# An expert layer on one NeuronCore: each group turned ahead of the output in front of it, and the last four results of a call copied by VectorE

## The chip, the cores and the metric

The kernel runs on one core of a Trainium2 chip. The metric is the device time of one execution in microseconds (us). Before the change it was 627.59 us, the median of three runs (627.01 to 629.43).

## What is computed

A block of six residual steps on x of shape (2, 1024, 128): a gated feed-forward, a softmax attention with eight heads, the feed-forward again, an expert layer, a linear attention (a delta scan with decay), and the expert layer again. The change touches the expert layer, which runs twice:

```python
logits = (x_flat @ Wr + br) / max(ROUTER_TEMP, 1e-06)
probs = jax.nn.softmax(logits, axis=-1)
topk_w, topk_idx = jax.lax.top_k(probs, TOP_K)
topk_w = topk_w / jnp.clip(jnp.sum(topk_w, axis=-1, keepdims=True), 1e-09)
h = jnp.einsum('nc,ech->neh', x_flat, W1) + b1
h = _layernorm(h, g1, be1)
h = jax.nn.gelu(h, approximate=False)
expert_out = jnp.einsum('neh,eho->neo', h, W2) + b2
sel = jnp.take_along_axis(expert_out, topk_idx[:, :, None], axis=1)
y_flat = jnp.sum(sel * topk_w[:, :, None], axis=1)
```

There are 16 experts, each token goes to 2 of them, and every width is 128.

## The kernel before

The two expert layers are called m3 (before the linear attention) and m5 (behind it, the last thing in the kernel). Each works on two halves of the tokens, m3[0] and m3[1], m5[0] and m5[1]. A half goes through these steps.

GpSimd scatters the half's rows by expert into a buffer in HBM, rows_in (16 indirect DMAs, `moe_pool_send`). SyncE loads the sorted rows in 8 groups (`moe_sync_load`). A group is 4 tiles of 128 rows, the eighth of a half has 3. The 16 groups of a call (both halves) are numbered u = 0 to 15 here. When all 8 groups of a half are stored to rows_out in HBM, GpSimd gathers the results with 16 indirect DMAs (`moe_pool_fetch`, line L1130), and VectorE adds them to x (`moe_vector_add`, L1369 and L1374), in four quarters that each wait for their 4 gathers.

For one group the engines do this, and each step waits for the one above it:

- PE `turn_in(u)` (L1174): 4 transposes of the loaded rows. ACT `rows(u)` (L1263) copies them out of PSUM.
- PE `hidden(u)` (L1191, L1193): a bias matmul and the first expert matrix. ACT `squares(u)` (L1270).
- DVE `summed`, `rstds`, `scaled` (L1327, L1338 with a chain of small operations, L1346): two groups share one chain of small operations: 0, then 1 and 2, ..., 13 and 14, then 15 alone.
- PE `turn(u)` (L1201): 4 transposes of the normalised group. ACT `gelu(u)` (L1280): 4 activations.
- PE `out(u)` (L1214, L1216): a bias matmul and the second expert matrix. ACT `out_in(u)` (L1289) copies the result out of PSUM, and ACT `store(u)` (L1154) issues its DMA to rows_out.

The order on each engine is written out by hand. PE does, for u = 0 to 12, `turn(u)`, `turn_in(u+4)`, `hidden(u+3)`, `out(u)`, and at the end 

```python
            turn(last - 3)
            turn(last - 2)
            out(last - 3)
            turn(last - 1)
            out(last - 2)
            out(last - 1)
```

ACT does `gelu(u)`, `store(u-1)`, `rows(u+4)`, `squares(u+3)`, `out_in(u)`. PSUM has 8 banks: 2 for turned-in rows, 4 for hidden groups, 1 for turned groups (TURN_BANK), 1 for outputs (OUT_BANK). Behind the groups of m3, VectorE runs `behind_m3`: the adds of m3[0] and the statistics for the linear attention. The first step of the linear attention on PE is L1484 (transposes of x; the second four wait for all four quarters of the adds of m3[0]), then L1491 and L1499. Behind the groups of m5, VectorE adds m5[0] and then m5[1], and SyncE stores x.

Of the kernel before, what the change touches and what calls it, by code (L numbers as in the profile page):

```python
# [20 lines left out]
P = 128  # L21
# [36 lines left out]
def build(nc, A):  # L58
    with ExitStack() as ctx:
# [3 lines left out]
        def sem(name):  # L63
            return ctx.enter_context(nc.semaphore(name))
# [842 lines left out]
        LEAD = 3  # L907
# [60 lines left out]
        class t:  # L968
# [1 line left out]
            xt, xtc = sem("t_rows_turned"), sem("t_rows_in")  # L970
            h, sq, sqr = sem("t_hidden"), sem("t_squared"), sem("t_squares_summed")
            z, zt, ac = sem("t_normed"), sem("t_normed_turned"), sem("t_gelu")
            y, yc = sem("t_out"), sem("t_out_copied")
            ys = [sem(f"t_out_stored{k}") for k in range(4)]
            yg = [sem(f"t_out_gathered{k}") for k in range(4)]

        def tiles_in(g):
            return min(4, NTL - 4 * (g % NGR))
# [170 lines left out]

        def moe_scalar_store(act, m, g):  # L1150
            b, u = m.b, NGR * m.i + g
            act.wait_ge(t.yc, u + 1)
# [10 lines left out]
        def moe_tensor(pe, pair, between):  # L1163
# [33 lines left out]
            def turn(u):  # L1197
                g = (u - u0) % NGR
                pe.wait_ge(t.z, u + 1)
                for j in range(tiles_in(g)):  # L1200
                    ins = pe.transpose(ps[:, turn_bank(last - u), j * P:(j + 1) * P], t_z[:, u % 4, j, :], cc("ident"))  # L1201
                ins.then_inc(t.zt, 1)

            def out(u):
                m, g = pair[(u - u0) // NGR], (u - u0) % NGR
                k = tiles_in(g)
                pe.wait_ge(t.ac, u + 1)
                bank = out_bank(last - u)
                if u == last - 1:
                    pe.wait_ge(t.yc, u - 1)  # L1210
                elif u >= u0 + 1 and u != last - 2:
                    pe.wait_ge(t.yc, u)
# [18 lines left out]
                hidden(u)  # L1231
                between(u - u0)
            routed(pair[1])
            for u in range(u0, last - LEAD):
                turn(u)
                if u + LEAD + 1 < last:
                    turn_in(u + LEAD + 1)
                hidden(u + LEAD)
                out(u)
            turn(last - 3)  # L1240
            turn(last - 2)
            out(last - 3)
            turn(last - 1)
            out(last - 2)
            out(last - 1)

        def turn_bank(left):

            return TURN_IN_BANKS[0] if left == 2 else TURN_BANK

        def out_bank(left):
            return TURN_IN_BANKS[1] if left == 2 else OUT_BANK

        def moe_scalar(act, pair, between):
            u0 = NGR * pair[0].i
# [28 lines left out]
            def out_in(u):  # L1284
                k = tiles_in(u)
                act.wait_ge(t.y, u + 1)
                if u >= 4:
                    act.wait_ge(t.ys[u % 4], 16 * (u // 4))
                nc.scalar.activation(t_y[:, u % 4, 0:k, :], ps[:, out_bank(last - u), 0:P * k].rearrange("p (j f) -> p j f", f=P), ACT.Copy)\  # L1289
                    .then_inc(t.yc, 1)  # L1290

            for u in range(u0, u0 + LEAD + 1):
                rows(u)
# [15 lines left out]
            gelu(last - 3)  # L1309
            store(last - 4)  # L1310
            gelu(last - 2)
            out_in(last - 3)
            gelu(last - 1)
            store(last - 3)
            out_in(last - 2)
            store(last - 2)
            out_in(last - 1)
            store(last - 1)

        def moe_vector_tiles(dve, vs, pair, behind):  # L1320
            u0 = NGR * pair[0].i

            def summed(u):
                k = tiles_in(u)
                dve.wait_ge(t.sq, u + 1)
                at, pos = place(u)
                nc.vector.tensor_reduce(t_ss[:, at, pos:pos + k], t_sq[:, u % 2, 0:k, :], AX.X, ALU.add).then_inc(t.sqr, 1)  # L1327

            def place(u):

# [20 lines left out]
            for u in range(u0 - 1, last + 1, 2):  # L1351
# [893 lines left out]
        def _(pe):  # L2245
# [48 lines left out]
            pe.wait_ge(t.yc, 2 * NGR)  # L2294

            def turned_before(g):
                pe.wait_ge(l.y, 2)
# [93 lines left out]
```

## Time and profile before

| | |
|---|---|
| median of 3 runs | 627.59 us (627.01 to 629.43) |
| the profiled execution: its own time, its span | 628.28 us, 626.1 us |
| PE busy | 512.6 us (82%) |
| VectorE busy | 484.3 us (77%) |
| ScalarE busy | 327.0 us (52%) |
| GpSimd busy | 142.0 us (23%) |
| groups of m3, from the first `turn` to the end of the last `out` | 350.1 to 407.1 us of the span |
| groups of m5, likewise | 537.9 to 595.5 us of the span |

The profiled execution's time is 2.18 us more than its span, and 0.69 us above the median. In the rows below "ACTq" and "SPq" are DMA issues on ScalarE's and SyncE's sequencers, "PEclk" is the granted clock of TensorE as a share of 2.4 GHz, and the square bracket at the end of a row is the idle time of the engine in front of it and what ended that.

### The profile page before, as it was taken

What the parts mean: (1) busy time and instruction counts of PE and PEld (TensorE: products, weight loads), DVE (VectorE), ACT (ScalarE), POOL (GpSimd) and SP (SyncE); (2) the same over time, 40 slices, a digit from 0 to 9 for tenths busy, and PEclk for the clock granted to TensorE, in tenths of its full rate; (3) what the DMA queues carried; (4) which work ended last, traced back from release to release, by engine and by line L of the source; (5) the groups of instructions that cost most, each with busy time, mean ns of one, the idle gap of its engine ahead of it and who ended that gap; (6) DMA issues with size and microseconds to landing.
All of it is one profiled execution on the core that took longest, in us unless ns stands there. A gap on an engine that the chain in (4) does not pass through costs nothing.

```text
span 626.1 us, 9476 instructions
## 1 busy us (share of the span) xinstructions
PE 512.6 (82%) x3033; PEld 270.7 (43%) x3033; DVE 484.3 (77%) x1373; ACT 327.0 (52%) x645; POOL 142.0 (23%) x188
## 2 busy tenths in 40 slices
PE   7687979989999999899585899877797786899800
PEld 3452322322223222244252777665555454777600
DVE  6997989898888998686987666897888758666722
ACT  2345546866676676798132688744242102678700
POOL 3000020000000000000075703654000072713645
PEclk9776969999999999999786899998797878899955
DMA  5006400028815000000225295421000015273432
GB/s 202 1 1 157 91 1 1 18 67 152 248 65 136 3 1 2 1 3 2 76 106 157 87 276 154 122 64 34 2 2 1 0 58 152 70 215 85 132 95 67
DMA packets 55981, 48.62 MB, mean 78 GB/s; under 512 B 5758, under 2 KB 48190, under 8 KB 55678
## 3 DMA queue, kind: packets, MB, share of 16 engines
q1 hardware_dynamic: 35326, 31.31, 18.4%
q0 software_dynamic: 4224, 8.59, 4.8%
q10 hardware_dynamic: 16384, 8.13, 4.5%
q8 instruction: 25, 0.41, 0.3%
q14 instruction: 22, 0.18, 0.1%
HBM read 24.94 MB, written 20.60 MB: 73 GB/s over the span
## 4 chain that ended last, share of the span: by engine, by line
PE 49%; DVE 25%; issue 9%; POOL 7%; ACT 4%; DMA 4%; SPq 1%; POOLq 0%; ACTq 0%; DVEq 0%
PE ps L747 7%; PE ps L716 7%; PE ps L737 7%; POOL rows_in L1105 5%; DVE arena L803 4%; PE ps L1193 4%; PE ps L1216 4%; POOL arena L1130 2%; PE ps L1555 2%; PE ps L1174 2%; PE ps L1201 2%; DVE stat L249 1%; ACT arena L1687 1%; PE ps L1499 1%; PE ps L545 1%
## 5 line engine op out<-in xcount | busy, mean ns | idle before, releaser
L803 DVE TENSOR_REDUCE arena<-ps 128x1 f32<-128x512 f32 x256 | 162.2, 682 | 25.4 <-PE ps L716 25.0
L869 ACT ACTIVATE arena<-ps 128x512 f32<-128x512 f32 x256 | 138.3, 603 | 58.5 <-PE ps L737 57.1
L716 PE MATMUL ps<-arena 96*128 96x512 bf16 x256 | 98.4, 397 | 7.9 <-DVE arena L803 6.8
L737 PE MATMUL ps<-arena 99*128 99x512 bf16 x256 | 96.4, 388 | 3.3 <-DMA arena<-arena 2.7
L1105 POOL DMA_INDIRECT rows_in<-xl,route x64 | 62.6, 978 | 149.9 <-DVE route L1061 131.6
L1130 POOL DMA_INDIRECT arena<-rows_out,route x64 | 61.3, 957 | 78.9 <-DMA rows_out<-arena 52.2
L747 PE MATMUL ps<-arena 128*32 128x512 f32 x512 | 68.2, 605 | 0.6 <-ACT arena L869 0.4
L737 PEld LDWEIGHTS ps<-arena 99*128 99x128 bf16 x256 | 24.9, 99 | 73.9 <-ACT arena L869 48.9
L716 PEld LDWEIGHTS ps<-arena 96*128 96x128 bf16 x256 | 25.1, 99 | 51.7 <-DVE arena L803 34.5
L1280 ACT ACTIVATE arena<-ps,route 128x128 f32<-128x128 f32 x124 | 46.4, 460 | 1.3 <-PE ps L1201 1.2
L1327 DVE TENSOR_REDUCE arena<-arena 128x4 f32<-128x512 f32 (+1 forms) x32 | 21.2, 663 | 30.4 <-ACT arena L1270 30.3
L884 POOL CAST arena<-arena 128x16 bf16<-128x16 f32 x7 | 1.4, 196 | 171.5 <-issue 148.4
L1193 PE MATMUL ps<-w,arena 128*128 x248 | 39.1, 303 | 0.0
L1216 PE MATMUL ps<-w,arena 128*128 x248 | 37.8, 297 | 0.0
L1193 PEld LDWEIGHTS ps<-w,arena 128*128 128x128 f32 x248 | 32.5, 204 | 7.9 <-issue 7.9
L1216 PEld LDWEIGHTS ps<-w,arena 128*128 128x128 f32 x248 | 31.7, 200 | 7.7 <-issue 7.7
L1289 ACT ACTIVATE arena<-ps 128x512 f32<-128x512 f32 (+1 forms) x32 | 18.7, 584 | 24.3 <-PE ps L1216 24.3
L280 ACT ACTIVATE xl<-x,small 128x128 f32<-128x128 f32 x40 | 16.4, 483 | 25.5 <-DVE small L266 25.5
L1369 DVE SCALAR_TENSOR_TENSOR x<-arena,route,x 128x128 f32<-128x128 f32 x32 | 9.8, 348 | 21.9 <-DMA arena<-rows_out,route 21.9
L203 PE MATMUL ps<-zerob 128*128 128x512 bf16 x77 | 25.0, 485 | 1.4 <-POOL zerob L1990 1.4
L1270 ACT ACTIVATE arena<-ps 128x512 f32<-128x512 f32 (+1 forms) x32 | 19.2, 599 | 13.2 <-PE ps L1193 13.0
L249 DVE BATCH_NORM_STATS2 stat<-x 128x6 f32<-128x128 f32 x96 | 20.1, 278 | 4.8 <-DMA x<-in_x 4.5
(283 smaller groups left out, 853.8 us busy)
## 6 DMA issues: line engine op xcount, KB each, us to landing
arena<-rows_in SPq DMA_DIRECT2D x28, 256.0 KB, 5.3
rows_out<-arena ACTq DMA_DIRECT2D x28, 256.0 KB, 2.5
rows_in<-zerob SPq DMA_DIRECT2D x2, 1920.0 KB, 11.2
arena<-att_parts SPq DMA_DIRECT2D x12, 256.0 KB, 8.7
arena<-in_consts SPq DMA_DIRECT2D x2, 1024.0 KB, 5.8
arena<-zerob SPq DMA_DIRECT2D x1, 2048.0 KB, 12.0
arena<-att_parts SPq DMA_DIRECT2D x14, 128.0 KB, 8.2
att_parts<-arena SPq DMA_DIRECT2D x6, 256.0 KB
```

What stands on the lines that cost most here:

```text
L203: pe.matmul(ps[:, bank, :], zerob[:, 0:P], zerob[:, :], start=True, stop=True)
L249: ins = nc.vector.bn_stats(stat[:, t, :], x[:, t, :])
L716: pe.matmul(ps[:, bank, :], a_qs[0:96, b, h, j * P:(j + 1) * P], a_ks[0:96, b, h, keys * 512:(keys + 1) * 512], start=True, stop=True).the ...
L737: pe.matmul(ps[:, score_bank(n), :], a_ks[0:99, b, h0 + h4, i * P:(i + 1) * P], a_qs[0:99, b, h0 + h4, half * 512:(half + 1) * 512], start ...
L747: ins = pe.matmul(ps[32 * h4:32 * h4 + 32, 4 + half, :], a_v[:, TB * b + i, h0 + h4, :], a_p[:, (4 * step + h4) % 16, :], start=(i == 0), ...
L803: nc.vector.tensor_reduce(a_nm[:, k % 2, o % 2, k // 2:k // 2 + 1], ps[:, bank, :], AX.X, ALU.max, negate=True).then_inc(a.mpu, 1)
L869: nc.scalar.activation(a_p[:, n % 16, :], ps[:, score_bank(n), :], ACT.Exp, scale=0.25).then_inc(a.ex, 1)
L1105: pool.indirect_dma_start(out=rows_in[b], out_offset=bass.IndirectOffsetOnAxis(ap=r_slot[b][:, k * TB + j:k * TB + j + 1], axis=0), in_=xl ...
L1130: pool.indirect_dma_start(out=t_yg[:, b, k, j, :], out_offset=None, in_=rows_out[b], in_offset=bass.IndirectOffsetOnAxis(ap=r_slot[b][:, k ...
L1193: ins = pe.matmul(ps[:, bank, j * P:(j + 1) * P], t_xt[:, u % 2, j * P:(j + 1) * P], w1[:, :, :].rearrange("c e f -> c (e f)")[:, bass.ds( ...
L1216: ins = pe.matmul(ps[:, bank, j * P:(j + 1) * P], t_a[:, u % 2, j * P:(j + 1) * P], w2[:, :, :].rearrange("c e f -> c (e f)")[:, bass.ds(a ...
L1280: ins = nc.scalar.activation(t_a[:, u % 2, j * P:(j + 1) * P], ps[:, turn_bank(last - u), j * P:(j + 1) * P], ACT.Gelu, bias=r_sel[m.b][:, ...
```

## The change

In both calls PE now turns a group ahead of the output in front of it: `turn(u)` comes before `out(u-1)`. From u = 2 on `hidden` runs one group further ahead than before (`ahead` gives the groups). In the last groups, transposes and outputs alternate between the two banks for turned and output groups and the two of the turned-in rows, which are free by then. ScalarE copies the results of groups 0 to 11, and VectorE those of groups 12 to 15, behind its last `scaled`. `turn` now also waits for the `gelu` that frees its bank.

```diff
-            y, yc = sem("t_out"), sem("t_out_copied")
+            y, yc_a, yc_v = sem("t_out"), sem("t_out_copied_by_scalar"), sem("t_out_copied_by_vector")
...
+        BY_VECTOR = [g >= 2 * NGR - 4 for g in range(2 * NGR)]
+        FREED = 1
...
             def turn(u):
                 g = (u - u0) % NGR
                 pe.wait_ge(t.z, u + 1)
+                if u > u0:
+                    pe.wait_ge(t.ac, u if last - u > 3 else u - 1)
...
-            for u in range(u0, last - LEAD):
+            for u in range(u0, last):
                 turn(u)
-                if u + LEAD + 1 < last:
-                    turn_in(u + LEAD + 1)
-                hidden(u + LEAD)
-                out(u)
-            turn(last - 3)
-            turn(last - 2)
-            out(last - 3)
-            turn(last - 1)
-            out(last - 2)
+                if u > u0:
+                    out(u - 1)
+                for v in ahead(u - u0):
+                    if v + 1 < 2 * NGR:
+                        turn_in(u0 + v + 1)
+                    hidden(u0 + v)
             out(last - 1)
 
+        def ahead(g):
+
+            first = g + LEAD + (1 if g > FREED else 0)
+            return range(first, min(g + LEAD + (1 if g >= FREED else 0), 2 * NGR - 1) + 1)
+
         def turn_bank(left):
 
-            return TURN_IN_BANKS[0] if left == 2 else TURN_BANK
+            return TURN_IN_BANKS[0] if left in (1, 3) else TURN_BANK
...
-            for u in range(u0, last - LEAD):
+            for u in range(u0, last):
                 gelu(u)
-                if u > u0:
-                    store(u - 1)
-                if u + LEAD + 1 < last:
-                    rows(u + LEAD + 1)
-                squares(u + LEAD)
-                out_in(u)
...
+                if u > u0 + 1:
+                    store(u - 2)
+                if u > u0 and not BY_VECTOR[u - 1 - u0]:
+                    out_in(u - 1)
+                for v in ahead(u - u0):
+                    if v + 1 < 2 * NGR:
+                        rows(u0 + v + 1)
+                    squares(u0 + v)
             store(last - 2)
-            out_in(last - 1)
             store(last - 1)
...
+            def out_in(u):
+                k = tiles_in(u)
+                dve.wait_ge(t.y, u + 1)
+                if u >= 4:
+                    dve.wait_ge(t.ys[u % 4], 16 * (u // 4))
+                nc.vector.tensor_copy(t_y[:, u % 4, 0:k, :], ps[:, out_bank(last + 1 - u), 0:P * k].rearrange("p (j f) -> p j f", f=P))\
+                    .then_inc(t.yc_v, 1)
...
+            for v in range(last - 3, last + 1):
+                out_in(v)
             behind()
```

PE before, around the output of group 6 in m3 (L1201 `turn`, L1174 `turn_in`, L1191 the first matmul of `hidden`, L1214 the first of `out`):

```order
L1201 MATMUL ps<-cst,arena 128x128 [waits t_normed]
L1201 MATMUL ps<-cst,arena 128x128 x3
L1174 MATMUL ps<-cst,arena 128x128 [waits t_rows_in,t_rows_loaded2]
L1174 MATMUL ps<-cst,arena 128x128 x3
...
L1191 MATMUL ps<-brow,pick 128x512 [waits t_normed,t_rows_in]
...
L1214 MATMUL ps<-brow,pick 128x512 [waits t_out_copied,t_gelu]
```

And of the change, around the output of group 6 (the lines are now L1214 `turn`, here of group 7, which has 3 tiles, L1225 `out`, L1185 `turn_in`, L1202 `hidden`):

```order
L1214 MATMUL ps<-cst,arena 128x128 [waits t_gelu,t_normed]
L1214 MATMUL ps<-cst,arena 128x128 x2
L1225 MATMUL ps<-brow,pick 128x512 [waits t_out_copied_by_scalar,t_gelu]
...
L1185 MATMUL ps<-cst,arena 128x128 [waits t_rows_in,t_rows_loaded4]
L1185 MATMUL ps<-cst,arena 128x128 x3
...
L1202 MATMUL ps<-brow,pick 128x512 [waits t_normed,t_rows_in]
```

The output of group 6 now stands behind the turn of group 7 and ahead of `turn_in(12)` and `hidden(11)`; one more `turn`, `turn_in` and `hidden` lie in front of it than before.

ACT before, from `gelu(7)` to the store of group 7, the last of the first half of m3 (L1280 `gelu`, L1154 `store`, L1263 `rows`, L1270 `squares`, L1289 `out_in`; the results of group 7 are 128x384):

```order
L1280 ACTIVATE arena<-ps,route 128x128 [waits t_out,t_normed_turned]
L1280 ACTIVATE arena<-ps,route 128x128 x2
L1154 DMA rows_out<-arena 128x4x128 [waits t_out_copied]
L1263 ACTIVATE arena<-ps 128x512 [waits t_hidden,t_rows_turned]
L1270 ACTIVATE arena<-ps 128x512 [waits t_squares_summed,t_hidden]
L1289 ACTIVATE arena<-ps 128x384 [waits t_out_stored3,t_out]
L1280 ACTIVATE arena<-ps,route 128x128 [waits t_out,t_normed_turned]
L1280 ACTIVATE arena<-ps,route 128x128 x3
L1154 DMA rows_out<-arena 128x3x128 [waits t_out_copied]
```

And of the change, from `gelu(8)` to the store of group 7 (L1293 `gelu`, L1165 `store`, L1302 `out_in`, L1276 `rows`, L1283 `squares`):

```order
L1293 ACTIVATE arena<-ps,route 128x128 [waits t_out,t_normed_turned]
L1293 ACTIVATE arena<-ps,route 128x128 x3
L1165 DMA rows_out<-arena 128x4x128 [waits t_out_copied_by_scalar]
L1302 ACTIVATE arena<-ps 128x384 [waits t_out_stored3,t_out]
L1276 ACTIVATE arena<-ps 128x512 [waits t_hidden,t_rows_turned]
L1283 ACTIVATE arena<-ps 128x512 [waits t_squares_summed,t_hidden]
L1293 ACTIVATE arena<-ps,route 128x128 [waits t_out,t_normed_turned]
L1293 ACTIVATE arena<-ps,route 128x128 x3
L1165 DMA rows_out<-arena 128x3x128 [waits t_out_copied_by_scalar]
```

The store of group 7 stood directly behind the four activations that follow its copy, `gelu(8)`; now `rows`, `squares` and the whole of `gelu(9)` stand between the copy and the store.

DVE of the change, at the end of the groups of m3 (L1361 is `scaled(15)`, L1341 the new copies, L1386 the first adds of m3[0]):

```order
L1361 TENSOR_TENSOR arena<-ps,arena 128x384 [waits t_normed_turned,vector_steps]
L1341 COPY arena<-ps 128x512 [waits t_out_stored0,t_out]
L1341 COPY arena<-ps 128x512 [waits t_out_stored1,t_out]
L1341 COPY arena<-ps 128x512 [waits t_out_stored2,t_out]
L1341 COPY arena<-ps 128x384 [waits t_out_stored3,t_out]
L1386 SCALAR_TENSOR_TENSOR x<-arena,route,x 128x128 [waits t_out_gathered0,e_gate]
```

Before, the adds followed `scaled(15)` at once; now four copies, which wait for outputs 12 to 15, stand between them.

## Rows read from the trace of the kernel before

**Rows 1.** Busy time per engine and PE clock: m3 steady, two linear attention stretches.

```profile
368.70:391.30 22.60, 22.37 (x156) 17.52 (x155) 14.44 (x54) 18.10 (x43) 4.70 (x5) 1.00 0.71 212
...
418.00:424.00 6.00, 6.00 (x33) 4.04 (x33) 5.76 (x13) 3.71 (x9) 4.48 (x6) 1.00 0.18 46
...
427.00:431.00 4.00, 4.00 (x21) 4.00 (x22) 1.43 (x6) 1.36 (x2) 3.08 (x4) 0.57 0.19 49
```

**Rows 2.** Timeline of PE, one steady group of m3: start, us, line, operation.

```profile
388.57 0.60 PE L1201 MATMUL ps<-cst,arena 128*128 128x128 f32 x4
389.01 0.60 PE L1174 MATMUL ps<-cst,arena 128*128 128x128 f32 x4
389.54 0.38 PE L1191 MATMUL ps<-brow,pick 24*128 24x512 bf16 x1
...
390.95 0.39 PE L1214 MATMUL ps<-brow,pick 24*128 24x512 bf16 x1
...
392.26 0.62 PE L1201 MATMUL ps<-cst,arena 128*128 128x128 f32 x4
```

**Rows 3.** Timeline of PE, end of m3 and start of the linear attention.

```profile
398.10 0.39 PE L1214 MATMUL ps<-brow,pick 24*128 24x512 bf16 x1 [0.47 <-ACT arena L1280]
...
401.83 0.38 PE L1214 MATMUL ps<-brow,pick 24*128 24x512 bf16 x1 [1.00 <-ACT arena L1280]
...
403.97 0.55 PE L1201 MATMUL ps<-cst,arena 128*128 128x128 f32 x3 [0.67 <-DVE arena L1346]
...
408.72 0.66 PE L1484 MATMUL ps<-cst,x 128*128 128x128 f32 x4 [0.37 <-DVE x L1374]
```

**Rows 4.** Timeline of DVE, end of m3: last scaling, first adds.

```profile
403.36 0.56 DVE L1346 TENSOR_TENSOR arena<-ps,arena 128x384 f32<-128x384 f32 x1
403.84 0.65 DVE L1369 SCALAR_TENSOR_TENSOR x<-arena,route,x 128x128 f32<-128x128 f32 x2
```

**Rows 5.** Timeline of ACT, m3: the store of group 7, then groups 13 and 15.

```profile
381.81 0.37 ACTq L1154 DMA_DIRECT2D rows_out<-arena  x1
...
403.34 0.60 ACT L1289 ACTIVATE arena<-ps 128x512 f32<-128x512 f32 x1 [0.17 <-PE ps L1216]
404.56 0.46 ACT L1280 ACTIVATE arena<-ps,route 128x128 f32<-128x128 f32 x1 [0.62 <-PE ps L1201]
404.57 0.37 ACTq L1154 DMA_DIRECT2D rows_out<-arena  x1
```

**Rows 6.** Timeline of POOL: first and last of m3[0]'s 16 gathers, last of m5[0]'s, first of m5[1]'s.

```profile
385.38 0.98 POOL L1130 DMA_INDIRECT arena<-rows_out,route  x1 [25.07 <-DMA rows_out<-arena]
...
404.17 0.95 POOL L1130 DMA_INDIRECT arena<-rows_out,route  x1 [0.30 <-issue]
...
591.94 0.94 POOL L1130 DMA_INDIRECT arena<-rows_out,route  x1 [0.30 <-issue]
601.30 0.95 POOL L1130 DMA_INDIRECT arena<-rows_out,route  x1 [8.42 <-issue]
```

**Rows 7.** The chain that ended last, in order of time: start, us, what.

```profile
410.06 1.96 PE ps L1491 x16
...
443.19 2.75 PE ps L1491 x16
...
596.01 2.59 DMA rows_out<-arena
...
598.75 2.56 issue
...
620.08 2.50 DMA arena<-rows_out,route
```

**Rows 8.** Timeline of PE: front of m3, `turn_in(8)` of m5, two waits in the linear attention.

```profile
351.13 0.38 PE L1191 MATMUL ps<-brow,pick 24*128 24x512 bf16 x1
...
355.40 0.60 PE L1201 MATMUL ps<-cst,arena 128*128 128x128 f32 x4
...
417.54 0.41 PE L1507 MATMUL ps<-route,cst 128*128 128x64 f32 x2 [1.77 <-ACT route L1669]
...
426.98 3.68 PE L1536 MATMUL ps<-arena 128*128 128x128 f32 x16 [2.66 <-ACT arena L1692]
...
555.61 0.66 PE L1174 MATMUL ps<-cst,arena 128*128 128x128 f32 x4 [0.87 <-DMA arena<-rows_in]
```

More of the change, by code:

```diff
@@ L972, in build, with wait_out_in @@
             z, zt, ac = sem("t_normed"), sem("t_normed_turned"), sem("t_gelu")
-            y, yc = sem("t_out"), sem("t_out_copied")
+            y, yc_a, yc_v = sem("t_out"), sem("t_out_copied_by_scalar"), sem("t_out_copied_by_vector")
             ys = [sem(f"t_out_stored{k}") for k in range(4)]
             yg = [sem(f"t_out_gathered{k}") for k in range(4)]
+        BY_VECTOR = [g >= 2 * NGR - 4 for g in range(2 * NGR)]
+        FREED = 1
+        def wait_out_in(eng, u):
+            done = (BY_VECTOR * (u // (2 * NGR)) + BY_VECTOR)[:u + 1]
+            if BY_VECTOR[u % (2 * NGR)]:
+                eng.wait_ge(t.yc_v, done.count(True))
+            else:
+                eng.wait_ge(t.yc_a, done.count(False))
         def tiles_in(g):
@@ L1151, in moe_scalar_store @@
             b, u = m.b, NGR * m.i + g
-            act.wait_ge(t.yc, u + 1)
+            wait_out_in(act, u)
             k = tiles_in(g)
@@ L1208, in out @@
                 bank = out_bank(last - u)
[L1209 to L1212, printed above, removed]
+                if u > u0 and last - u != 3:
+                    wait_out_in(pe, u - 1 if last - u > 2 else u - 2)
                 regs, at = where.pop(u)
@@ L1233, in moe_tensor @@
             routed(pair[1])
-            for u in range(u0, last - LEAD):
+            for u in range(u0, last):
                 turn(u)
-                if u + LEAD + 1 < last:
-                    turn_in(u + LEAD + 1)
-                hidden(u + LEAD)
-                out(u)
-            turn(last - 3)
-            turn(last - 2)
-            out(last - 3)
-            turn(last - 1)
-            out(last - 2)
+                if u > u0:
[4 more added lines that the diff above has]
+                    hidden(u0 + v)
             out(last - 1)
+        def ahead(g):
+            first = g + LEAD + (1 if g > FREED else 0)
+            return range(first, min(g + LEAD + (1 if g >= FREED else 0), 2 * NGR - 1) + 1)
         def turn_bank(left):
-            return TURN_IN_BANKS[0] if left == 2 else TURN_BANK
+            return TURN_IN_BANKS[0] if left in (1, 3) else TURN_BANK
         def out_bank(left):
-            return TURN_IN_BANKS[1] if left == 2 else OUT_BANK
+            return TURN_IN_BANKS[1] if left in (1, 3) else OUT_BANK
         def moe_scalar(act, pair, between):
@@ L1289, in out_in @@
                 nc.scalar.activation(t_y[:, u % 4, 0:k, :], ps[:, out_bank(last - u), 0:P * k].rearrange("p (j f) -> p j f", f=P), ACT.Copy)\
-                    .then_inc(t.yc, 1)
+                    .then_inc(t.yc_a, 1)
             for u in range(u0, u0 + LEAD + 1):
@@ L1299, in store @@
                 moe_scalar_store(act, pair[(u - u0) // NGR], (u - u0) % NGR)
-            for u in range(u0, last - LEAD):
+            for u in range(u0, last):
                 gelu(u)
-                if u > u0:
-                    store(u - 1)
-                if u + LEAD + 1 < last:
-                    rows(u + LEAD + 1)
-                squares(u + LEAD)
-                out_in(u)
[L1309 to L1315, printed above, removed]
+                if u > u0 + 1:
[6 more added lines that the diff above has]
+                    squares(u0 + v)
             store(last - 2)
-            out_in(last - 1)
             store(last - 1)
@@ L2293, in _ @@
             moe_tensor(pe, m3, between_m3)
-            pe.wait_ge(t.yc, 2 * NGR)
+            wait_out_in(pe, 2 * NGR - 1)
             def turned_before(g):
```

## The prediction, made before the changed kernel was run

> **What bounds the kernel now.** I read the chain that ended last first. Its end is the gather of m5[1], issued by GpSimd when the last store of m5 has landed [rows 7]. So in m5 only the moment of the last store counts. Then I read the engines' timelines over both calls. In the steady part of m3 PE is busy for 22.37 of 22.60 us at full clock [rows 1]: the bound is TensorE's own work. A group takes it 3.69 us: `turn` 0.44, `turn_in` 0.53, `hidden` 1.41, `out` 1.31, each from its start to the start of the next step [rows 2]. Reordering that work gives nothing there. PE waits only at the ends: 0.47, 1.00 and 0.67 us in the last groups of m3 [rows 3], and in m5 0.87 us for the rows of its second half, in front of `turn_in(8)` [rows 8].
>
> Behind m3 two other things end last. The second L1484 waits for the adds of m3[0], which run from 403.84 to 408.72 [rows 3, 4] beside PE's last outputs. And the last gather of m3[0] is issued at 404.17 [rows 6] and lands about 2.5 later [rows 7], at 406.7, less than 1 us before the fourth quarter of those adds starts (three quarters of 1.22 us behind 403.84, at 407.5). The gather's issues follow the store of group 7: store at 381.81 [rows 5], first gather at 385.38 [rows 6].
>
> **The store of group 7 comes later, and the gather with it (m3, +3.6).** Ahead of `out(7)` PE now also does `turn(8)`, `turn_in(12)` and `hidden(11)`: 0.44 + 0.53 + 1.41 = 2.38. Behind it the store waits until `gelu(9)` starts, which needs `turn_in(13)`, `hidden(12)` and `turn(9)`: another 2.38. Before, it waited for its own copy, some 0.5 (a copy of 512 columns takes 0.60 [rows 5]). In front, `turn(1)` now meets a wait for the scaling of group 1, which I put at 0.3 by the same kind of row in the tail (0.67 [rows 3]); below nothing it can't be. Sum 2.38 + 2.38 − 0.5 + 0.3 = 4.6, less some 0.2 of small waits for scalings that the longer lead removes: +4.4. GpSimd's 16 issues move as a block, so the last is at 408.6 and lands at 411.1. The last quarter of the adds takes 1.22 and ends at 412.3, against 408.72 now: **+3.6**.
>
> Does the store really wait for `gelu(9)`? It needs only its copy, and the row decides. The copy of group 13 ended at 403.34 + 0.60 = 403.94, but its store was issued at 404.57, together with the start of `gelu(15)` at 404.56, which stands ahead of it and had waited for PE [rows 5]. So a store is held by a wait of the activation in front. The Trainium skill says otherwise (Perfetto Trace Analysis, "DVE / Act Engine Instruction"): an instruction is pushed into a wait queue, and the sequencer is free for the next. By that rule the store would leave with its copy, the gather would end some 2 us earlier, and the sum would be that of rival C; the trace does not agree with it here.
>
> **The tail of the groups (m3: hidden; m5: +0.4).** `hidden(14)` has one `turn` and one `out` less in front (1.75), less 0.3 in front: the last scaling of m3 comes 1.4 earlier, ending at about 402.5 (403.92 now [rows 4]). But `store(12)` now stands ahead of `gelu(15)`, and waits for VectorE's copy of group 12, which begins only behind that last scaling: copy 0.6 plus issue 0.37, then `gelu(15)`. So `gelu(15)` starts 1.07 behind the scaling; before it was 404.56 − 403.92 = 0.64. The last output gains 1.4 − 0.4 = 1.0 in m3 and ends near 406.0 instead of about 407.1. VectorE then copies it (0.6 by ScalarE's row; VectorE's own reading of PSUM, 0.56 for 384 columns, is as long [rows 4, 5]), to 406.6, and begins the adds 2.8 later than now. Three quarters are done at 410.3, so the fourth still waits for the gather's 411.1. The late copies cost nothing only under the cover of the late gather; without it the adds would end at 406.6 + 4.88 = 411.5, +2.8.
>
> In m5 the gain isn't there. Its `turn_in(8)` stands 1.75 earlier in PE's order but can't start before its rows come, at 555.61, since those depend on GpSimd's scatter, which nothing here moves. Against m3 everything behind is 1.4 late: the last scaling comes when it does now, the last output 0.4 later, and the last store **+0.4**. The gathers of m5[0] shift by 4.4 + 1.4 = 5.8, the last from 591.94 to 597.7, and GpSimd is free again at about 599.0, while the last store's landing (598.6 now, 596.01 + 2.59 [rows 7]) would be at 599.0. The two meet; I add nothing. There is a 2.56 us idle stretch on GpSimd in front of its first gather of m5[1], with no releaser [rows 7]. I leave it in the sum.
>
> **The clock (+2.3).** Both longer waits of PE may drop its clock. In m5 the wait in front of `turn_in(8)` grows from 0.87 to about 2.3. Behind a wait of 2.66 the granted clock was 0.57 for 4 us, which is mostly the 1.2 GHz level; behind one of 1.77 it stayed at 1.00, 2.4 GHz [rows 1, 8]. The price is seen at the front of m3, where a `hidden` and an `out` took 355.40 − 351.13 = 4.27 at the low level against 1.41 + 1.31 = 2.72: **+1.55**. 2.3 is nearer to 2.66, so I take it; at the other end it is nothing. Behind m3, PE now has only four transposes to do between 406.0 and 412.3, where before it worked through. L1491 took 2.75 at the low level and 1.96 at the full one [rows 7]: **+0.8**, between 0 and 1.6 if L1499 is slow too. The Trainium skill (TensorE: Matmul & The Clock Gate, "HAM oscillation") tells of a kernel whose every wait for a load makes the next tile start at the slow clock. By that rule both waits cost, and the sum stays as here; by the 1.77 row neither does, which is rival B.
>
> **Sum.** 3.6 + 0.8 + 0.4 + 1.55 = 6.35, call it 6.3. All that follows m3 hangs on L1484 (PE, then VectorE, then GpSimd's scatter), so the first two terms pass to the end. The profiled execution's span of 626.1 becomes 632.4, its time 628.28 becomes 634.6; at the median of the runs, 627.59 + 6.3 = **633.9 us**.
>
> **The rivals.**
> - A, the forecast (0.50): 633.9. Its own range is 631.5 to 636.5, for landings of 2.1 to 3.4 instead of 2.5 and clock terms of 1.5 to 3.2.
> - B, the clock stays up at both places (0.17): 3.6 + 0.4 = 4.0, 631.6. For it speaks the 1.77 row, against it the 2.66 row.
> - C, the store of group 7 isn't held (0.07): the gather shifts by 2.7 alone, and the adds, held by VectorE's late copies, end +2.8. Sum 5.5, 633.1.
> - D, GpSimd's 2.56 us stretch disappears in m5 (0.14). It then comes straight from the gathers of m5[0] instead of from idleness; if the stretch is work that fits between, up to 2.5 come back: 631.4 with the clock terms, 629.1 without.
> - E, faster (0.06): the steady group is not PE's pure work but the ring PE, `gelu`, `out`, copy, which just fits. Turning ahead opens that ring. Place: 13 groups in each of 2 calls. To be over 0.5% faster, 3.1 us beyond the 6.3 to be made good, each of the 26 would have to shrink by 0.36, to 3.33; if the 0.5 us that PE's sum could at most hide vanished, it would be 13 us less, 621. Against it: PE shows no idle row in the steady part, 22.37 of 22.60.
> - F, more is lost than I see (0.06): 637 and above, a transfer or a clock drop in the linear attention.
>
> **How the numbers follow.** What a measurement here can tell from no change is about 0.5%, 3.1 us: below 624.5 is faster, above 630.7 slower. Slower hold A, C, F, nearly all of B and half of D: 0.50 + 0.07 + 0.06 + 0.13 + 0.07 = 0.83. I take 0.05 off for an m3 term half as large in case B, so 0.78. The same: the rest of B and D, 0.11, and most of those 0.05: 0.15. Faster: E, and 0.01 for gains I don't see: 0.07. The range goes from 629.1 (D without the clock) to 637.0 (A's end and half a microsecond), and leaves out E, F and the edge of D.
>
> **What the profile of the change should show.** In m3 the first gather at about 389.8, the second L1484 at 412.3, waiting for DVE's last add, and that add waiting for a DMA; PE's waits in the tail shorter than 1.00. In m5 a wait for the rows of about 2.3 in front of `turn_in(8)`, then a clock below 1.00 for some 4 us; the last store some 40.8 us behind the start of `turn_in(8)` (596.01 − 555.61 = 40.4 now [rows 7, 8]), or 42.4 with the clock down. The store of a group together with the start of the `gelu` two groups on. I am wrong if the steady group becomes shorter than 3.6, if L1484 comes before 411, or if GpSimd's first gather of m5[1] follows the landing of the last store at once.

## The result, and where the time went

The change took 636.08 us, median of four runs (631.89 to 638.15), beside 628.51 for the kernel before (four runs, 627.01 to 630.51). The ratio is 1.0102, with a 95% interval of 1.0063 to 1.0141: slower, by 7.6 us. The prediction was 633.9 with a range of 629.1 to 637.0. The profiled execution took 635.05 us, with a span of 633.2 against 626.1. The 7.1 us between the spans are accounted for below. A few executions lie over 1.5% above the fastest one of their kernel; they count in the medians below and not in the ratios.

The steady part first: two `turn` of m3 that follow each other, then busy times and clock of PE in the order "PE, PEld, DVE, ACT, POOL, PEclk, DMA share, GB/s".

```profile
370.62 0.60 PE L1214 MATMUL ps<-cst,arena 128*128 128x128 f32 x4
374.31 0.60 PE L1214 MATMUL ps<-cst,arena 128*128 128x128 f32 x4
```

```profile
372.00:395.00 23.00, 23.00 (x163) 17.93 (x162) 15.26 (x58) 18.64 (x45) 4.95 (x6) 1.00 0.49 150
```

A group still takes 3.69 us, as in [rows 2], and PE has no gap now. The difference comes from the ends of the two calls. The first `turn` of m3 starts at 350.51, against 350.13 before, so nearly 0.4 us of the shifts in m3 are there ahead of anything that the change moves.

**End of m3: +2.5.** The store of group 7 on ScalarE, then GpSimd's first and last gather of m3[0], and the first of m3[1]:

```profile
385.23 0.60 ACT L1283 ACTIVATE arena<-ps 128x512 f32<-128x512 f32 x1 [0.60 <-PE ps L1204]
385.68 0.37 ACTq L1165 DMA_DIRECT2D rows_out<-arena  x1
385.72 1.50 ACT L1293 ACTIVATE arena<-ps,route 128x128 f32<-128x128 f32 x4
```

```profile
388.53 0.98 POOL L1141 DMA_INDIRECT arena<-rows_out,route  x1 [29.79 <-DMA rows_out<-arena]
...
407.38 0.95 POOL L1141 DMA_INDIRECT arena<-rows_out,route  x1 [0.30 <-issue]
409.15 0.94 POOL L1141 DMA_INDIRECT arena<-rows_out,route  x1 [0.82 <-DMA rows_out<-arena]
```

The copy of group 7 had begun at 383.63 and its store left at 385.68, together with `gelu(9)` at 385.72: 3.87 later than in [rows 5]. The gathers are 3.2 later than in [rows 6]. VectorE's timeline shows what that does to the adds (L1361 the last scaling, L1341 the new copies, L1386 the first instructions of each quarter of the adds):

```profile
401.02 0.56 DVE L1361 TENSOR_TENSOR arena<-ps,arena 128x384 f32<-128x384 f32 x1
401.50 1.28 DVE L1341 COPY arena<-ps 128x512 f32<-128x512 f32 x2
403.82 0.69 DVE L1341 COPY arena<-ps 128x512 f32<-128x512 f32 x1 [1.05 <-PE ps L1227]
405.18 0.56 DVE L1341 COPY arena<-ps 128x384 f32<-128x384 f32 x1 [0.66 <-PE ps L1227]
405.65 0.60 DVE L1386 SCALAR_TENSOR_TENSOR x<-arena,route,x 128x128 f32<-128x128 f32 x2
...
409.91 0.61 DVE L1386 SCALAR_TENSOR_TENSOR x<-arena,route,x 128x128 f32<-128x128 f32 x2 [0.65 <-DMA arena<-rows_out,route]
```

The last scaling comes 2.3 earlier than in [rows 4], but the adds begin 1.8 later, behind the copies, and their fourth quarter waits another 0.65 for the last gather. PE, from there into the linear attention:

```profile
408.23 0.63 PE L1501 MATMUL ps<-cst,x 128*128 128x128 f32 x4 [3.09 <-DVE x L1391]
411.23 1.11 PE L1501 MATMUL ps<-cst,x 128*128 128x128 f32 x4 [2.37 <-DVE x L1391]
413.03 3.59 PE L1508 MATMUL ps<-w,xt 128*128 128x16 f32 x16 [0.69 <-ACT xt L1679]
...
430.98 2.05 PE L1553 MATMUL ps<-arena 128*128 128x128 f32 x16 [2.67 <-ACT arena L1709]
```

The second L1501 (L1484 before) starts at 411.23, against 408.72 in [rows 3]: +2.5. L1508 then takes 3.59 instead of the 1.96 of [rows 7]; the granted clock is 0.50 there. By L1553 the shift has grown to 4.0 (430.98 against 426.98). But L1553 takes 2.05 where it took 3.68 [rows 8], so 1.6 are given back, and the shift that leaves the linear attention is 2.3 to 2.5.

**m5: +4.6 more.** `turn_in(8)` and the clock behind it, in the views of PE and of windows (busy times as above):

```profile
558.58 0.66 PE L1185 MATMUL ps<-cst,arena 128*128 128x128 f32 x4 [3.92 <-DMA arena<-rows_in]
...
600.43 0.39 PE L1225 MATMUL ps<-brow,pick 24*128 24x512 bf16 x1
```

```profile
559.00:563.00 4.00, 4.00 (x16) 2.61 (x14) 0.55 (x1) 1.82 (x5) 0.00 (x0) 0.52 1.06 293
563.00:567.00 4.00, 4.00 (x21) 3.25 (x21) 0.00 (x0) 1.96 (x5) 0.00 (x0) 0.63 0.51 133
567.00:592.00 25.00, 25.00 (x178) 19.53 (x177) 16.27 (x61) 19.87 (x48) 5.05 (x6) 1.00 0.30 83
```

PE waits 3.92 us for its rows instead of 0.87 [rows 8], and then runs at or near the 1.2 GHz level for some 7 us. The chain that ended last, at its end:

```profile
602.31 3.41 DMA rows_out<-arena
...
605.87 2.56 issue
...
627.16 2.52 DMA arena<-rows_out,route
```

`turn_in(8)` is 2.97 later than before: 2.26 from in front (GpSimd's last scatter of rows leaves at 552.84, before at 550.58), and 0.78 because that scatter takes 3.06 to land instead of 2.28, less 0.06 in the load behind it. The last store stands 43.73 behind it, before 40.40 [rows 7, 8]: +3.33. Its landing takes 3.41 instead of 2.59: +0.82. Together 7.1, the whole difference of the spans.

### The profile page after: what moved, and what is told of

Read it like the earlier page. It is cut to its first block, busy times and chain, and to the rows that moved or that the text cites. A ratio compares the mean times of both kernels' runs of the same rounds, so it can differ in the third digit from the quotient of the medians.

```text
span 633.2 us, 9503 instructions
## 1 busy us (share of the span) xinstructions
PE 515.5 (81%) x3030; PEld 273.3 (43%) x3033; DVE 489.0 (77%) x1381; ACT 322.7 (51%) x637; POOL 141.7 (22%) x188
## 4 chain that ended last, share of the span: by engine, by line
PE 46%; DVE 22%; issue 10%; POOL 10%; DMA 5%; ACT 4%; SPq 2%; POOLq 0%; ACTq 0%; DVEq 0%
PE ps L747 7%; PE ps L737 6%; PE ps L716 6%; POOL rows_in L1116 5%; POOL arena L1141 4%; DVE arena L803 4%; PE ps L1204 4%; PE ps L1227 3%; PE ps L1572 2%; PE ps L545 2%; PE ps L1185 2%; PE ps L1516 1%; PE ps L1202 1%; ACT arena L1704 1%; PE ps L1214 1%
## 5 line engine op out<-in xcount | busy, mean ns | idle before, releaser
L1293 ACT ACTIVATE arena<-ps,route 128x128 f32<-128x128 f32 x124 | 46.6, 459 | 4.4 <-PE ps L1214 4.3
L1227 PE MATMUL ps<-w,arena 128*128 x248 | 37.1, 293 | 0.0
L1283 ACT ACTIVATE arena<-ps 128x512 f32<-128x512 f32 (+1 forms) x32 | 18.7, 584 | 31.6 <-PE ps L1204 31.6
L1227 PEld LDWEIGHTS ps<-w,arena 128*128 128x128 f32 x248 | 30.9, 195 | 7.5 <-issue 7.5
L1185 PE MATMUL ps<-cst,arena 128*128 128x128 f32 x124 | 22.0, 308 | 7.1 <-DMA arena<-rows_in 7.0
L1276 ACT ACTIVATE arena<-ps 128x512 f32<-128x512 f32 (+1 forms) x32 | 19.0, 595 | 13.4 <-PE ps L1185 13.4
L203 PE MATMUL ps<-zerob 128*128 128x512 bf16 x74 | 24.2, 490 | 1.6 <-POOL zerob L2007 1.4
L1386 DVE SCALAR_TENSOR_TENSOR x<-arena,route,x 128x128 f32<-128x128 f32 x32 | 9.8, 348 | 19.5 <-DMA arena<-rows_out,route 19.5
```

The source lines that it names most:

```text
L203: pe.matmul(ps[:, bank, :], zerob[:, 0:P], zerob[:, :], start=True, stop=True)
L1185: ins = pe.transpose(ps[:, TURN_IN_BANKS[u % 2], j * P:(j + 1) * P], t_xg[:, m.b, g, j, :], cc("ident"))
L1293: ins = nc.scalar.activation(t_a[:, u % 2, j * P:(j + 1) * P], ps[:, turn_bank(last - u), j * P:(j + 1) * P], ACT.Gelu, bias=r_sel[m.b][:, ...
```

## The experiments

Twelve kernels ran. The first eight came out some 90 to 100 us longer than the runs above, the kernel before beside them too (726.96 and 721.01 us, medians of 19 and 23 runs). Nearly all of that lies behind 320 us, in the two expert calls (their routing included) and the linear attention. These are called the long conditions below. Their times are compared with the kernel before beside them, and within their traces. The last four ran with the kernel before at 629.2 and 630.0.

| kernel | us | ratio to before (95%) |
|---|---|---|
| store behind its copy | 733.51 | 1.0145 (1.0045 to 1.0245) |
| all copies by ScalarE | 722.26 | 0.9974 (0.9926 to 1.0022) |
| lead raised at 4 | 730.24 | 1.0094 (1.0057 to 1.0132) |
| filler in the wait | 733.02 | 1.0121 (1.0004 to 1.0239) |
| the change again | 722.70 | 1.0057 (1.0023 to 1.0090) |
| all copies by ScalarE, again | 718.51 | 0.9979 (0.9946 to 1.0013) |
| lead raised at 9 | 733.38 | 1.0183 (1.0121 to 1.0245) |
| lead at 9, ScalarE copies, store behind | 729.96 | 1.0140 (1.0094 to 1.0186) |
| the kernel before, as a null test | 629.82 | 1.0007 (0.9976 to 1.0039) |
| old order, last two copies by VectorE | 634.92 | 1.0088 (1.0058 to 1.0118) |
| filler in the wait, again | 635.47 | 1.0082 (1.0051 to 1.0113) |
| ScalarE copies, store behind | 636.76 | 1.0066 (1.0025 to 1.0108) |

**1. Each store directly behind its copy.**

```diff
-                if u > u0 + 1:
+                if u > u0 + 1 and BY_VECTOR[u - 2 - u0]:
                     store(u - 2)
                 if u > u0 and not BY_VECTOR[u - 1 - u0]:
                     out_in(u - 1)
+                    store(u - 1)
```

> The changed kernel, with each store that ScalarE's copies feed issued directly behind its copy instead of one group later. Theory 1 (mine: the store of group 7 is held by the turn and gelu of group 9): it leaves at 384.1 instead of 385.68, the gathers of m3[0] move up by 1.5, and the adds of m3[0] are then held by VectorE's late copies alone: the second transposes of the linear attention start 0.65 earlier, the end about 0.7 earlier. In m5 the gathers of m5[0] end 1.5 earlier, which can spare the last store some of its slower landing (3.41): up to 0.8 more. Theory 2 (the gather is not what is late in m3): no change of the second transposes at all, total within 0.5.

The time tells nothing at this size. ScalarE's timeline shows the order at work:

```profile
404.20 0.62 ACT L1302 ACTIVATE arena<-ps 128x512 f32<-128x512 f32 x1
404.85 0.37 ACTq L1165 DMA_DIRECT2D rows_out<-arena  x1
405.31 0.60 ACT L1276 ACTIVATE arena<-ps 128x512 f32<-128x512 f32 x1 [0.50 <-ACT arena L1302]
```

The store leaves 0.65 behind the start of its copy, which is as soon as the copy is done, and ScalarE starts nothing for 0.50 behind the copy while the store is issued. In the change the store stood behind `gelu(9)` and left with it. So a store in ScalarE's order is held by what stands ahead of it, and holds what stands behind. Whether its gain reaches the second transposes is read in experiment 8.

**2. All copies by ScalarE,** the order kept.

```diff
-        BY_VECTOR = [g >= 2 * NGR - 4 for g in range(2 * NGR)]
+        BY_VECTOR = [False for g in range(2 * NGR)]
...
             store(last - 2)
+            out_in(last - 1)
             store(last - 1)
...
-            for v in range(last - 3, last + 1):
-                out_in(v)
```

> The changed kernel, with all 16 results of a call copied by ScalarE. Theory 1 (the gather covers the late copies but for 0.65): VectorE's adds start 4 us earlier, right behind its last scaling, but the last quarter still waits for the gather, so the second transposes start at most 0.2 earlier in m3. In m5 the store of group 12 no longer waits behind the last scaling, so gelu(15) starts 0.4 earlier and the last store too. Total 0.3 to 0.8 less than the changed kernel. Theory 2 (the copies by VectorE are the main loss): the second transposes 2 us earlier or more, total 2.5 less.

> All copies by ScalarE, the new order kept. Theory 1 (VectorE's copies are covered by the late gather, the fourth quarter of the adds waits for a DMA): the end moves by 0 to -0.8 us against the change. Theory 2 (the four copies delay VectorE's adds, and the adds are what PE waits for): -2.5 us or more. In the trace theory 1 wants the last add of m3[0] to wait for a DMA again, theory 2 no such wait and an earlier L1501. If the earlier -4 us against the others was only the spread of those runs, the time is within 1 us of the change.

Twice no slower than before, where the change beside the second is 1.0057 (experiment 5): the four copies cost some 0.8% of 720 there, by ratios whose intervals just part. The reason is in VectorE's rows. With the change:

```profile
429.67 0.56 DVE L1361 TENSOR_TENSOR arena<-ps,arena 128x384 f32<-128x384 f32 x1
...
437.11 0.56 DVE L1341 COPY arena<-ps 128x384 f32<-128x384 f32 x1 [0.49 <-PE ps L1227]
437.59 0.61 DVE L1386 SCALAR_TENSOR_TENSOR x<-arena,route,x 128x128 f32<-128x128 f32 x2
```

And with all copies by ScalarE (L1362 the last scaling, L1385 the adds):

```profile
437.85 0.56 DVE L1362 TENSOR_TENSOR arena<-ps,arena 128x384 f32<-128x384 f32 x1
438.32 0.60 DVE L1385 SCALAR_TENSOR_TENSOR x<-arena,route,x 128x128 f32<-128x128 f32 x2
```

The two traces are compared from the last scaling on, since the second is some 7 us late from in front of m3. In them the gathers of m3[0] were all issued by 423.1 (the change) and 431.3, long before the groups ended. The adds begin 7.9 us behind the last scaling with the change, 0.5 without the copies. Theory 2 holds here, where the gather is early; theory 1 holds in the run of the result, where the fourth quarter waited for a DMA. Both are one rule: the adds end by the later of the two, the copies or the last gather.

**3. The lead raised later.** FREED sets from which group on `hidden` runs one further ahead; first 4, then 9, instead of 1.

```diff
-        FREED = 1
+        FREED = 9
```

> The changed kernel, with the lead of the hidden groups raised at group 4 instead of group 1, so that PE does turn(4) and out(3) ahead of the turned-in rows of group 8, as before the change. Theory 1 (m5 loses because work that stood in front of the wait for the rows now stands behind it, and the longer wait drops the clock): the wait in front of turn_in(8) in m5 falls from 3.92 to 2.2, all behind it comes 1.75 earlier, m3 is unchanged: 1.75 less, and up to 3.1 more if the clock stays up. Theory 2 (the rows come late by themselves and the order of the work around them costs nothing): total as the changed kernel within 0.5.

> The lead of hidden is raised only at group 9 instead of group 2, so turn_in(12) and hidden(11) no longer stand ahead of out(7), and turn_in(8) stands one turn and one out later. Theory 1 (the order ahead of store 7 and ahead of turn_in(8) costs, with the clock drop behind a long wait): store 7 is 1.9 us earlier than in the change, the second L1501 earlier by 0.65 only, since VectorE's copies then hold the adds; the wait before turn_in(8) in m5 shrinks from 3.92 to about 2.2; the end comes 2.4 us earlier if the clock still drops as long, 5.5 us if it stays up: 630.5 to 633.5. Theory 2 (the cost lies in turning ahead itself and in the late copies, not in the raised lead): within 0.7 us of the change, and the wait before turn_in(8) shortens without the last store coming nearer.

With 4, the ratio is 1.0094, and m3 shows one wait of 1.09 for the scaling: no gain. With 9, a miss for both theories: 1.0183, some 9 us more than the change's 1.0057 beside it, where 2.4 to 5.5 less was expected; the intervals part, but leave some 5 us of doubt on the 9. The `turn` of four groups of m3, in PE's timeline with the lead raised at 9:

```profile
383.33 0.66 PE L1214 MATMUL ps<-cst,arena 128*128 128x128 f32 x4 [1.07 <-DVE arena L1361]
386.96 0.60 PE L1214 MATMUL ps<-cst,arena 128*128 128x128 f32 x4
391.88 0.65 PE L1214 MATMUL ps<-cst,arena 128*128 128x128 f32 x4 [1.30 <-DVE arena L1361]
395.62 0.60 PE L1214 MATMUL ps<-cst,arena 128*128 128x128 f32 x4
```

Every second group waits 1.07 to 1.30 for VectorE's scaling, four times in m3 (the sum over L1214 there is 4.8) and four times in m5 (0.70 to 1.30, 4.2): 9.0 in all, as much as the difference. The change has no such wait in these groups, neither in the result nor beside this run. Turning ahead of the output takes one `out` from between `hidden(u)` and `turn(u)`, and VectorE's chain for two groups needs that time; the raised lead pays for it. I had seen only the lead's price, not what it buys. Its price in m5 wasn't tested: in none of the first eight traces does PE wait for rows in front of `turn_in(8)` of m5, so what a later lead does to that wait stays open.

**4. Lead at 9, all copies by ScalarE, each store behind its copy** (the edits of 1, 2 and 3).

> Turning ahead kept, its three suspected costs taken away together: lead raised only at group 9, all copies by ScalarE, each store directly behind its copy. Theory 1: first gather of m3[0] at about 384.6 (388.53 in the change), the second L1501 some 3 to 4 us earlier, the last store of m5 another 2 to 5 us earlier with a wait before turn_in(8) of about 2: 627 to 631 us, so no slower than the kernel before. Theory 2 (turning ahead costs by itself, because the last groups then wait for scalings and for the gelu that frees the bank): 633 us or more.

1.0140: slower, as theory 2 said, but not for its reason. The waits for the scaling are there as in 3 (1.30, 1.17 and 1.31 in m3), so the missing lead costs more than the other two edits give, in these conditions.

**5. The kernel before, and the change again,** each as if new.

> The changed kernel once more, unaltered, as the base for the runs beside it, since the first four runs came out some 100 us longer than the two kernels of the result, the kernel before included. If this run is near 636 us again, differences to it can be read to about 1 us; if it is near 730 too, only the places inside the trace can be compared. Against the kernel before I expect 5 to 9 us more in either case (7.6 in the result).

> The kernel before, unaltered, run as if it were a new one: a null test of what the ratio can tell, and a trace of it under the conditions of the experiments, in which both kernels take some 90 to 100 us more than in the result. Ratio 1.000 within 0.005. The eight traces so far show, in the two expert calls, stretches of 3 to 16 us in which PE, ScalarE and VectorE all stand still while GpSimd issues its indirect DMAs, with no releaser. If these belong to the conditions and not to the change, this trace has them too, at the same places, and about as many; if they came from the change, it has few.

The change came out under the long conditions, the kernel before under the others, so their traces can't be compared. The change's 1.0057 is 4.1 us, a little under the 5 to 9 expected. What the long traces show is standstills. In that of the change, at one moment:

```profile
421.08 0.58 PE L1225 MATMUL ps<-brow,pick 24*128 24x512 bf16 x1 [8.32 <-issue]
...
420.34 0.60 ACT L1302 ACTIVATE arena<-ps 128x512 f32<-128x512 f32 x1 [8.35 <-remote]
...
426.50 0.55 DVE L1334 TENSOR_REDUCE arena<-arena 128x3 f32<-128x384 f32 x1 [12.07 <-ACT arena L1283]
```

All three engines stand still for 8 us, while GpSimd issues gathers at its usual pace (0.95 each, from 403.3 to 423.1). None of the traces at about 630 us, of either kernel, has such a row of over 2.5 us in the expert calls and the linear attention. For the kernel before against itself, 1.0007 within 0.0032 is what it should be.

**6. The old order, with the last two results copied by VectorE.** The edit splits the semaphore of the copies as the change does, and moves two copies behind `scaled`:

```diff
+        BY_VECTOR = [g >= 2 * NGR - 2 for g in range(2 * NGR)]
...
-            out_in(last - 2)
             store(last - 2)
-            out_in(last - 1)
             store(last - 1)
...
+            for v in range(last - 1, last + 1):
+                out_in(v)
             behind()
```

> The kernel before, its order untouched, but the last two results of each call (groups 14 and 15) copied by VectorE behind its last scaled, where the change has the last four. Theory 1 (without a late gather nothing covers these copies: VectorE's adds of m3[0] then wait for the last output): the adds of m3[0] start at the end of the last copy, about 3.8 us later than before, the second transposes of the linear attention too, and the whole is 3.5 to 4.3 us slower than the kernel before, ratio 1.005 to 1.007; nothing more comes in m5, where VectorE's adds of m5[0] are not on the path. Theory 2 (the cost of the change is the order alone, the copies are free wherever they stand): within 0.5 us of before, and PE's first wait in the linear attention is as short as before.

Measured +0.88%, 5.5 us, above the 3.5 to 4.3 expected. VectorE, with the edit:

```profile
404.12 0.56 DVE L1362 TENSOR_TENSOR arena<-ps,arena 128x384 f32<-128x384 f32 x1
406.73 0.69 DVE L1342 COPY arena<-ps 128x512 f32<-128x512 f32 x1 [2.05 <-PE ps L1226]
407.91 0.56 DVE L1342 COPY arena<-ps 128x384 f32<-128x384 f32 x1 [0.49 <-PE ps L1226]
408.39 0.60 DVE L1387 SCALAR_TENSOR_TENSOR x<-arena,route,x 128x128 f32<-128x128 f32 x2
```

And in the trace of the kernel before beside it:

```profile
404.81 0.56 DVE L1346 TENSOR_TENSOR arena<-ps,arena 128x384 f32<-128x384 f32 x1
405.28 0.60 DVE L1369 SCALAR_TENSOR_TENSOR x<-arena,route,x 128x128 f32<-128x128 f32 x2
```

From the last scaling to the adds 4.27 instead of 0.47: 3.8, as expected. PE's L1502 waits 3.09 and 1.26, and L1509 then takes 3.59 instead of 1.96, the clock's 1.6 on top, which the expectation had left out. Here nothing gives it back:

```profile
434.21 3.68 PE L1554 MATMUL ps<-arena 128*128 128x128 f32 x16 [2.67 <-ACT arena L1710]
```

L1554 takes 3.68, as L1536 does in [rows 8]. Theory 2 falls. In the old order late copies are expensive by themselves, 5.5 us for two.

**7. Filler in front of `turn_in(8)` of m5.**

```diff
-                pe.wait_ge(t.xg[g], 16 * (m.i + 1))
                 if u >= u0 + 2:
                     pe.wait_ge(t.xtc, u - 1)
+                if u == u0 + NGR and u0:
+                    keep_clock(pe, TURN_IN_BANKS[u % 2], 16)
+                pe.wait_ge(t.xg[g], 16 * (m.i + 1))
```

> The changed kernel, with 16 matmuls on zeros in m5 in front of the wait for the rows of group 8, into a bank that is free there. They take 16 x 0.215 = 3.4 us of the 3.92 that PE waits. Theory 1 (the low granted clock behind that wait costs 3.1): the granted clock stays at 1.00 from 559 to 567, the last store comes 3.1 earlier, the total is 3.1 less. Theory 2 (the clock is hidden by waits in the tail): the last store moves by under 1.

> The changed kernel, with 16 extra matmuls on zeros (128x512, about 3.5 us at the full clock) between hidden(6) and turn_in(8) of m5, into the bank that turn_in(8) is to use; the earlier trial of this came out under conditions in which that wait was not there. Theory 1 (the wait of 3.92 us in front of turn_in(8) drops the clock, and the low clock costs 3.1 us behind it): turn_in(8) starts where it does in the change, the clock stays at 1.00 behind it, the last store comes 40.6 us behind turn_in(8) instead of 43.7, and the whole is 3.1 us shorter, about 633 at the change's 636. Theory 2 (the low clock is in the shadow of the loads of rows that follow, since these arrive one after another): the clock stays up, and the last store moves by less than 1 us.

In the first trial the wait wasn't there, and nothing follows from it. In the second (L203 the filler, L1187 `turn_in`, L1227 the first matmul of `out`; below it the windows):

```profile
557.54 3.62 PE L203 MATMUL ps<-zerob 128*128 128x512 bf16 x16
560.99 0.60 PE L1187 MATMUL ps<-cst,arena 128*128 128x128 f32 x4
...
599.58 0.38 PE L1227 MATMUL ps<-brow,pick 24*128 24x512 bf16 x1
```

```profile
559.00:563.00 4.00, 4.00 (x25) 2.51 (x23) 1.99 (x7) 0.79 (x2) 0.00 (x0) 1.00 1.05 298
563.00:567.00 4.00, 4.00 (x29) 2.99 (x27) 0.55 (x1) 3.24 (x9) 0.00 (x0) 1.00 0.88 236
```

The clock stays at 1.00, and from `turn_in(8)` to `out(15)` it is 38.59 us, against 41.85 in the change (600.43 − 558.58): 3.26 for the low clock, since PE is busy for all of 559:567 in both traces and waits for nothing there. The last store stands 40.46 behind `turn_in(8)`, where theory 1 said 40.6. Theory 2 falls. But the whole is 1.0082 against 1.0102, with intervals that overlap, and not the 3.1 us less that theory 1 wanted, so a gain in time isn't shown. PE came to the wait later in this run, the load of rows was issued at 557.24 (555.91 in the change), and by the change's distance of 2.67 from that issue to `turn_in(8)` they were there at about 559.9, an estimate: the wait would have been 2.4, and the filler ran some 1.1 us too long.

**8. The new order, all copies by ScalarE, each store behind its copy** (the edits of 1 and 2, the lead as in the change).

> The changed kernel's order on PE kept whole, all copies by ScalarE, and each store directly behind its copy instead of behind the next group's gelu. Theory 1 (in m3 it is the late store of group 7 and then the late copies that hold VectorE's adds, so both must go): first gather of m3[0] 2.4 us earlier than the change's 388.5, adds no longer behind copies, the second transposes of the linear attention at about 408.5 instead of 411.2, the wait before turn_in(8) in m5 and the clock drop unchanged, the last store 0 to 1 us later: 2 to 3 us less than the change, 633 to 634, so still slower than the kernel before. Theory 2 (the copies and the order of the stores are covered in both calls, the raised lead alone costs): within 1 us of the change.

1.0066 with a wide interval (the medians stand 1.1% apart), and a profiled execution 3.4 us above its median, so I read distances only. From `turn(7)` of m3 the store of group 7 is 1.5 nearer than in the change (6.18 against 7.69), the first gather too (9.05 against 10.54), and the second transposes (31.69 against 33.24; 30.98 in the kernel before). VectorE's adds begin right behind the last scaling, and then stand 3.17 us for the gather:

```profile
405.23 0.60 DVE L1385 SCALAR_TENSOR_TENSOR x<-arena,route,x 128x128 f32<-128x128 f32 x2
...
412.02 0.61 DVE L1385 SCALAR_TENSOR_TENSOR x<-arena,route,x 128x128 f32<-128x128 f32 x2 [3.17 <-DMA arena<-rows_out,route]
```

So with the copies gone it is the gather alone, and the order on PE ahead of `out(7)` keeps that late. I had put both gains higher (2.4 and 2.7). Neither kernel is beaten by any of these.

## Why the prediction was right, and which of its terms were not

- **Sign, size and mechanism.** 633.9 was forecast and 636.08 measured: +6.3 against +7.6, inside the range. The causes are the ones named: the held store of group 7, the wait in front of `turn_in(8)`, the clock. That the sum comes so near is in part luck. Its m3 terms, 3.6 + 0.8 = 4.4, are 2 us too large against the 2.3 to 2.5 that leave the linear attention, and its m5 terms, 0.4 + 1.55 = 1.95, are 2.7 too small against 4.6.
- **Group 7 and its gather (+3.6, measured +2.5).** The store moved by 3.87 of the 4.4. `out(7)` starts 2.10 later (382.10 against 380.00) where 2.48 were put down; the wait of 0.3 put in front isn't in the trace. From there the store takes 3.58 instead of 1.81, 1.77 more of the 1.88 put down. The first gather came 2.85 behind the store, before 3.57: the gathers moved by 3.2. The rest, 0.7, is the slack that the last gather had. "The store waits for `gelu(9)`" is right: 385.68 and 385.72, and experiments 1 and 8 free it. Rival C falls. The second transposes, at 411.23, came only 0.2 behind the 411 at which the prediction called itself wrong.
- **The late copies.** "Covered by the late gather" is shown, to within 0.65 us. The size, +2.8, was not: the adds began 1.8 later, since the last scaling came 2.3 earlier and not 1.4. In the old order, where nothing moves the scaling, two such copies cost 3.8 and a clock drop (experiment 6).
- **Low clock behind m3 (+0.8, measured 1.6, then 0).** The upper end came true for L1508, and with the drop in m5 that ends rival B. What the step did not have is that the drop of [rows 8] later, at L1536, then stays away, and the 1.6 come back. The Trainium skill (TensorE: Matmul & The Clock Gate, "HAM oscillation") tells of a kernel in which each wait for a load makes the next tile start slow. The traces agree for the 3.92, and behind m3 from the second of two waits on (3.09, then 2.37), and not for the 2.67 in front of L1553. Much the same wait before the same instruction was followed by 3.68 us in the kernel before (3.52 in its trace beside experiment 6) and by 2.05 in the change and in experiments 7 and 8. A stretch at the low level not long ahead of it doesn't explain that: the change had one until shortly before 420, and experiment 6 had one until near 424 (L1509 took 3.59), and its L1554 still took 3.68. What decides it stays open. Without it the change would have come out near 637.7, beyond the range.
- **Order and tail of m5 (+0.4).** Experiment 7 gives it without the clock: 40.46 against 40.40 before. The step is right to 0.4 us: 1.75 more work behind `turn_in(8)`, and as much less waiting in the tail (0.17 and 0.35 are left of 0.47, 1.00 and 0.61).
- **The wait and the clock in m5 (+1.55, measured +3.3).** This is the term that was mis-sized most. The wait is 3.92 instead of 2.3, since PE came earlier and the rows 0.7 later by the scatter's longer landing, which was in no term; in experiment 8, with the same order on PE, it was 2.59, with the clock down behind it too. I took the price of one `hidden` and one `out` at the low level, about 4 us of it; it lasted some 7, at twice the price.
- **The landing (0 predicted, +0.82 measured)** was not in the sum at all.
- **Rival D falls.** The 2.56 us are there, in all six traces at about 630. The chain at the end of experiment 7 shows what they aren't:

```profile
603.72 0.33 POOL arena L1141
...
604.14 2.56 issue
606.70 1.04 POOL arena L1141
```

Here the last gather of m5[0] was still under way on GpSimd (0.95 from 603.72) when the store landed; the stretch runs from the landing all the same, beside the gather's end.

- **Rival E falls,** the steady group being 3.69 as before. But something like its idea, that a ring of engines just fits, is true for the ring through VectorE: experiment 3 shows that with one `out` less in it PE waits some 1.2 in every second group.

## What to carry to other kernels

A store or copy that another engine waits for should be costed with all that stands ahead of it in its own engine's order, waits included, and a late copy with all that stands behind it. Where a wait grows, ask how long the low clock lasts behind it, not only whether it comes: here the low clock behind the wait for rows took 3.3 us, read from distances within the traces. And before a lead is taken back as a cost, look for the wait that it hides.

## What the hardware showed that I had not expected

- The last store of m5 took 2.59 us to land in both traces of the kernel before, 2.08 in experiment 6, 2.60 with the filler (601.45 to 604.05), 3.41 in the change and 4.54 in experiment 8, each read from one execution. GpSimd's gathers ran beside it with the filler too, so they alone don't explain it. This stays open.
- Under the conditions of the first eight kernels PE, ScalarE and VectorE stood still for 3 to 16 us at a time, nearly always from a moment in which GpSimd was issuing indirect DMAs (in the change's trace of experiment 5 there are eight such stretches, of 20 to 22 us). What holds them is not settled; no trace of the kernel before was taken under them.
